# Gated cross-attention and sign FFN: row vectors and gates loaded to every partition by DMA in place of one-row products on TensorE

## The chip, the cores and the metric

One core of one Trainium2 chip runs the kernel. The metric is the device time of one execution in microseconds (us); less is better. The engines are TensorE (PE), VectorE (DVE), ScalarE (ACT), GpSimd (POOL) and SyncE (SP, which only issues transfers here); each runs its own instructions in order and meets the others at semaphores.

## The reference

x is 16 batches of 128 rows of 256 values, ctx has the same shape, all float32. A mask marks keys to leave out.

```python
def block(x, ctx, mask, g_xattn, g_ffn, Wq, bq, Wk, bk, Wo, bo, W, scale, bias):
    q = layernorm(x) @ Wq.T + bq
    k = ctx @ Wk.T + bk
    s = where(mask, -inf, q @ k.T)                 # one head, 128 x 128 per batch
    a = softmax(s) @ ctx                           # the values are ctx itself
    x = x + tanh(g_xattn[0]) * (a @ Wo.T + bo)
    w = where(W >= 0, 1, -1)
    y = clip(layernorm(x) @ w.T * scale + bias, -100, 100)
    return x + tanh(g_ffn[0]) * y
```

The change is about the five small operands: the gates g_xattn and g_ffn (one value each) and the rows bo, scale and bias (256 values each). Each of them is needed in all 128 partitions.

## The kernel before, in words

The 16 batches are worked on in 8 groups of two (G = 8, GB = 2); "(g)" behind a name means group g. Everything stays in SBUF. Each engine's program is written out by hand in one block, so the order on an engine is the order of the code, and a wait holds up everything behind it on that engine.

Set-up. The query and key weights are multiplied into one 256 x 256 matrix (wqk), so that K = wqk applied to ctx is all that the scores need from ctx. wo is transposed on PE and multiplied by tanh(g_xattn) on eviction (woT_hi on ACT, L245; woT_lo on DVE, L478, which waits for woT_hi), so that Z = ctx @ woT replaces the values. The FFN weights become signs with their mean taken off (w_cent, DVE, L495 to L502), and PE transposes them. Operands marked hi and lo are two parts of one float32 value, whose products are added up.

Each group then goes through: transposes of ctx (cT, L533, with the eviction cT_hi on ACT L200 and cT_lo on DVE L380), statistics of x (bn_x, DVE L362, and mv_x, L366), normalisation on POOL (xn, L304), its transposes (xT), K (L538, evicted to K_sb on ACT, L210), Z (L538), scores (a product that lays the mask, L595, then L600), the negated maximum on DVE (nmax, L395), exp on ACT (L221), transposes of p (L608, copied to PT_sb by ACT, L226), attend (L619), the residual on DVE (x1, L405, which the profile lists as x_sb), its statistics and transposes (x1T), the FFN product (L538 into ps_F), scaling on DVE (f_scaled, L413), bias and clip on POOL (f_biased L322, f_clip), and the last addition on DVE.

PE's program, which sets the order around the change: 18 warm-up transposes, the product of the two weights, transpose_ctx(0), the key bias, transpose_x(0), project_K(0), the gate product (L656), the transposes of wo, the bo product (L660). Then for i = 0 to 6: scores(i), transpose_ctx(i+1), transpose_x1(i-1) from i = 1 on, transpose_x(i+1), project_Z(i), project_K(i+1), transpose_p(i), then for i = 0 the transposes of w_cent and the scale and bias products (L675, L676), for later i ffn(i-1), and last attend(i).

The small operands. ACT issues eight loads at its start: bq, bk, the mask, two gates, bo, scale and bias, the last five to partition 0 alone. To bring them to all partitions, PE multiplies a row of 128 ones (ones_1) with each: the gates into o_bank, bo into x1T_bank, scale and bias into the two halves of f_bank. ACT takes them from there: tanh_g (L242), bo_g (L247, times tanh), sc_g and bi_g (L261, L262). Since these products borrow banks that have other uses, there are waits for that too: attend(0) for tanh_ready, the transposes of w_cent for bo_g_ready, the scale product for woT_lo_ready, and ffn(0) for bi_g_ready.

DVE's program around the change: after the set-up of wqk come the statistics of groups 1, 2 and 3, then woT_lo, four operations on one column each that make the clip limits (L480 to L485), and the loop: max_of_scores(0) (nmax), split_cT(1), the w_cent sequence. ACT's: K_sb(0), tanh_g, woT_hi, bo_g, and the loop: cT_hi(1), exp(0), xT(1), Z_sb(0), PT_sb(0), K_sb(1), wT, sc_g, bi_g. POOL waits for bo_g before its first xb = x + bo_g (L316).

SP issues its loads in this order: wq, wk, x(0), ctx(0), x(1), wo, ctx(1), w, and then x and ctx of groups 2 to 7, 256 KB each; later the stores.

Of the kernel before, what the change touches and what calls it, by code (L numbers as in the profile page):

```python
# [21 lines left out]
def gated_xattn_ffn(nc, x, ctx, mask, g_xattn, g_ffn, wq, bq, wk, bk, wo, bo, w_ffn, scale_ffn, bias_ffn, out):  # L22
# [25 lines left out]
    with ExitStack() as stack:  # L48
# [6 lines left out]
        def bank(name):  # L55
# [51 lines left out]

        gate_row, bo_row, sc_row, bi_row = sb("gate_row", [1, 2]), sb("bo_row", [1, D]), sb("sc_row", [1, D]), sb("bi_row", [1, D])
        tanh_g, neg_g, abs_g = sb("tanh_g", [P, 2]), sb("neg_g", [P, 1]), sb("abs_g", [P, 1])
# [7 lines left out]
        sel = sb("sel", [P, G, P], BF16)  # L117
        ones_1 = sb("ones_1", [1, P])

        x_loaded, ctx_loaded = [sem(f"x_loaded{g}") for g in range(G)], [sem(f"ctx_loaded{g}") for g in range(G)]  # L120
        wq_loaded, wk_loaded, bq_loaded, bk_loaded, wo_loaded, w_loaded, gate_loaded, rows_loaded, mask_loaded, stored = (
            sem(n) for n in ("wq_loaded", "wk_loaded", "bq_loaded", "bk_loaded", "wo_loaded", "w_loaded", "gate_loaded",
                             "rows_loaded", "mask_loaded", "stored"))

# [5 lines left out]
                             "wqk_lo_ready"))  # L130
        ps_gate_ready, tanh_ready, ps_rows_ready, ps_bo_ready, bo_g_ready, sc_g_ready, bi_g_ready = (
            sem(n) for n in ("ps_gate_ready", "tanh_ready", "ps_rows_ready", "ps_bo_ready", "bo_g_ready", "sc_g_ready",
                             "bi_g_ready"))
        neg_g_done, abs_g_done, clip_ready = (sem(n) for n in ("neg_g_done", "abs_g_done", "clip_ready"))
# [24 lines left out]
        def _(sp):  # L159
# [11 lines left out]
            sp.dma_start(wo_sb[:], wo.rearrange("(c p) d -> p c d", p=P)).then_inc(wo_loaded, 16)  # L171
            load_ctx(1)
            sp.dma_start(w_sb[:], w_ffn.rearrange("(c p) d -> p c d", p=P)).then_inc(w_loaded, 16)
            for g in range(2, G):
                load_x(g)
                load_ctx(g)
            for g in range(G - 2):
                sp.wait_ge(out_done, g + 1)
                sp.dma_start(out_rows[:, rows(g), :], out_sb[:, rows(g), :]).then_inc(stored, 16)
# [9 lines left out]
        def _(act):  # L189
# [3 lines left out]
            for k, v in enumerate((g_xattn, g_ffn)):  # L193
                act.dma_start(gate_row[:, k:k + 1], row(v)).then_inc(gate_loaded, 16)
            for tile, v in ((bo_row, bo), (sc_row, scale_ffn), (bi_row, bias_ffn)):
                act.dma_start(tile[:], row(v)).then_inc(rows_loaded, 16)

# [42 lines left out]
            evict_K(0)  # L240
            act.wait_ge(ps_gate_ready, 1)
            nc.scalar.activation(tanh_g[:], o_bank[:, 0:2], ACT.Tanh).then_inc(tanh_ready, 1)  # L242
            act.wait_ge(tanh_ready, 1)
            act.wait_ge(ps_woT_ready, 1)
            nc.scalar.activation(woT_hi[:], ps_woT, ACT.Identity, scale=tanh_g[:, 0:1]).then_inc(woT_hi_ready, 1)  # L245
            act.wait_ge(ps_bo_ready, 1)
            nc.scalar.activation(bo_g[:], x1T_bank[:, 0:D], ACT.Identity, scale=tanh_g[:, 0:1]).then_inc(bo_g_ready, 1)  # L247
            for i in range(G - 1):
                evict_cT_hi(i + 1)
                exp(i)  # L250
                if i >= 1:
                    evict_x1T_hi(i - 1)
                evict_xT(i + 1)
                evict_Z(i)
                evict_PT(i)
                evict_K(i + 1)
                if i == 0:
                    act.wait_ge(ps_wT_ready, 1)
                    nc.scalar.copy(wT[:], ps_x1T).then_inc(wT_ready, 1)
                    act.wait_ge(ps_rows_ready, 1)  # L260
                    nc.scalar.activation(sc_g[:], f_bank[:, 0:D], ACT.Identity, scale=tanh_g[:, 1:2]).then_inc(sc_g_ready, 1)  # L261
                    nc.scalar.activation(bi_g[:], f_bank[:, D:2 * D], ACT.Identity, scale=tanh_g[:, 1:2]  # L262
                                         ).then_inc(bi_g_ready, 1)
# [9 lines left out]
        def _(pool):  # L273
            nc.gpsimd.memset(ident[:], 0.0).then_inc(zeroed, 1)
            nc.gpsimd.memset(half[:], -0.5).then_inc(consts_ready, 1)
            nc.gpsimd.memset(ones_1[:], 1.0).then_inc(consts_ready, 1)
            pool.wait_ge(zeroed, 1)
# [50 lines left out]

            pool.wait_ge(consts_ready, 2)
            offsets_x(0)  # L330
# [26 lines left out]
        def _(dve):  # L357
# [49 lines left out]

            def scale_ffn_out(g):
                dve.wait_ge(rstd_1_done, g + 1)
                dve.wait_ge(F_prod, g + 1)  # L410
                for b in range(GB):
                    r = g * GB + b
                    nc.vector.scalar_tensor_tensor(out=f_scaled[:, r], in0=ps_F[:, b], scalar=rstd_1[:, r:r + 1],  # L413
                                                   in1=sc_g[:], op0=ALU.mult, op1=ALU.mult).then_inc(f_scaled_done, 1)
# [113 lines left out]
        def _(pe):  # L528
# [82 lines left out]
            def attend(g):  # L611
                pe.wait_ge(PT_done, g + 1)
                pe.wait_ge(Z_done, g + 1)
                if g >= 1:
                    pe.wait_ge(x1_done, GB * g)
                else:
                    pe.wait_ge(tanh_ready, 1)
                for b in range(GB):
                    last = nc.tensor.matmul(ps_O[:, b], PT_sb[:, g % 2, b], Z_sb[:, g % 2, b], start=True, stop=True)  # L619
                last.then_inc(O_prod, 1)  # L620

            def ffn(g):
# [3 lines left out]
                else:  # L626
                    pe.wait_ge(bi_g_ready, 1)
                for b in range(GB):
# [6 lines left out]
            pe.wait_ge(ident_ready, 1)  # L635
            pe.wait_ge(consts_ready, 2)
            for _ in range(WARM_UP):
# [16 lines left out]
            project_K(0)  # L654
            pe.wait_ge(gate_loaded, 32)
            nc.tensor.matmul(o_bank[:, 0:2], ones_1[:], gate_row[:], start=True, stop=True).then_inc(ps_gate_ready, 1)  # L656
            pe.wait_ge(wo_loaded, 16)
            transposes(ps_woT, wo_sb).then_inc(ps_woT_ready, 1)
            pe.wait_ge(rows_loaded, 48)
            nc.tensor.matmul(x1T_bank[:, 0:D], ones_1[:], bo_row[:], start=True, stop=True).then_inc(ps_bo_ready, 1)  # L660
            for i in range(G - 1):
# [8 lines left out]
                if i == 0:  # L670
                    pe.wait_ge(bo_g_ready, 1)
                    pe.wait_ge(w_cent_ready, DC)
                    transposes(ps_x1T, w_cent).then_inc(ps_wT_ready, 1)
                    pe.wait_ge(woT_lo_ready, 1)
                    nc.tensor.matmul(f_bank[:, 0:D], ones_1[:], sc_row[:], start=True, stop=True)  # L675
                    nc.tensor.matmul(f_bank[:, D:2 * D], ones_1[:], bi_row[:], start=True, stop=True).then_inc(ps_rows_ready, 1)  # L676
                else:
# [53 lines left out]
```

## Time and profile before

| | |
|---|---|
| median of 3 runs | 81.14 us (80.91 to 81.71) |
| the profiled execution, its own time | 81.19 us |
| its span, first to last instruction | 79.3 us |
| PE busy | 69.3 us |
| DVE, POOL, ACT busy | 56.1, 55.0, 36.6 us |
| granted TensorE clock, mean over the span | 0.970 of full speed |

All times in the rows count from the start of the span. In the chain, a piece is as long as it carried the chain, so that overlapping instructions of one engine aren't counted twice; "issue" is time in which nothing shown was waited for. In a timeline, a row merges instructions of one kind that follow each other (x2, x4), its second number is the time from the first's start to the last's end, and the brackets hold the engine's idle time ahead of it and what ended it.

### The profile page before, as it was taken

Reading aid. Unit: us, or ns where it says so; the run is one execution under the profiler, and the core shown is the slowest. Engines: PE = TensorE matmul, PEld = TensorE weight load, DVE = VectorE, ACT = ScalarE, POOL = GpSimd, SP = SyncE. Lnnn points to the kernel's source line nnn. Section 1 sums busy time; section 2 is a strip of 40 time slices with the busy share of each in tenths; the row PEclk is TensorE's granted clock in tenths of the full one; section 3 lists DMA queues with packets and bytes.
Section 4 is the critical chain, followed back from the end, with each engine's and each line's share of the span. In section 5 each row is a group of like instructions: output and inputs, shape, how many; then the busy total and the mean of one; then the engine's idle time right before and its main releaser. Section 6 shows DMA issues by size and latency. Waiting matters only on the chain.

```text
span 79.3 us, 1567 instructions
## 1 busy us (share of the span) xinstructions
PE 69.3 (87%) x522; PEld 64.8 (82%) x522; DVE 56.1 (71%) x163; ACT 36.6 (46%) x99; POOL 55.0 (69%) x102
## 2 busy tenths in 40 slices
PE   2999899999999999999999999999999899865000
PEld 2998797986999899989999998999899798654000
DVE  2494976890469489929966980896498359899980
ACT  0054257748386529435850945394267525330000
POOL 6006576989406508889999988999999994528930
PEclk9999999999999999999999999999999999999755
DMA  2899999980000000040003003000300300300025
GB/s 22 265 368 351 351 349 348 348 254 0 0 4 0 0 0 8 0 134 2 0 4 132 8 0 132 0 0 0 132 0 8 111 22 0 119 13 0 0 72 192
DMA packets 7713, 7.44 MB, mean 94 GB/s; under 512 B 791, under 2 KB 7450, under 8 KB 7706
## 3 DMA queue, kind: packets, MB, share of 16 engines
q1 hardware_dynamic: 7376, 7.34, 28.7%
q8 instruction: 4, 0.07, 0.4%
q10 hardware_dynamic: 330, 0.01, 0.2%
q14 instruction: 3, 0.02, 0.1%
HBM read 5.25 MB, written 2.10 MB: 93 GB/s over the span
## 4 chain that ended last, share of the span: by engine, by line
PE 73%; DVE 12%; DMA 4%; ACT 3%; POOL 3%; issue 2%; DVEq 0%; POOLq 0%
PE ps_K L538 14%; PE ps_Z L538 14%; PE ps_S L600 9%; PE ps_O L619 8%; PE ps_F L538 8%; PE ps_xT L533 5%; PE ps_x1T L533 4%; PE ps_cT L533 4%; DMA wq_sb<-in_L_xattn_Wq_dram 4%; PE ps_S L608 2%; DVE f_biased L439 2%; DVE out_sb L444 2%; DVE f_last L441 1%; POOL xn L304 1%; DVE f_scaled L436 1%
## 5 line engine op out<-in xcount | busy, mean ns | idle before, releaser
L405 DVE SCALAR_TENSOR_TENSOR x_sb<-ps_O,recip_p,xb_sb 128x256 f32<-128x256 f32 x14 | 6.1, 480 | 11.1 <-PE ps_O L619 11.1
L322 POOL TENSOR_TENSOR f_biased<-f_scaled,bi_g 128x256 f32<-128x256 f32 x14 | 10.0, 733 | 3.4 <-DVE f_scaled L413 3.3
L316 POOL TENSOR_TENSOR xb_sb<-x_sb,bo_g 128x256 f32<-128x256 f32 x16 | 11.4, 729 | 0.8 <-ACT bo_g L247 0.8
L200 ACT CAST cT_hi<-ps_cT 128x512 fp32r<-128x512 f32 x8 | 4.7, 586 | 13.5 <-PE ps_cT L533 13.4
L304 POOL TENSOR_SCALAR xn<-x_sb,rstd_x,off_x 128x256 f32<-128x256 f32 x16 | 9.9, 626 | 0.5
L538 PE MATMUL ps_Z<-woT_hi,cT_hi 128*128 128x256 f32 x32 | 9.7, 305 | 0.0
L538 PE MATMUL ps_K<-cT_hi,wqk_hi 128*128 128x256 f32 x32 | 9.1, 283 | 0.0
L538 PE MATMUL ps_K<-cT_hi,wqk_lo 128*128 128x256 f32 x32 | 9.0, 282 | 0.0
L538 PE MATMUL ps_K<-cT_lo,wqk_hi 128*128 128x256 f32 x32 | 9.0, 282 | 0.0
L538 PE MATMUL ps_Z<-woT_lo,cT_hi 128*128 128x256 f32 x32 | 9.0, 281 | 0.0
L538 PE MATMUL ps_Z<-woT_hi,cT_lo 128*128 128x256 f32 x32 | 9.0, 281 | 0.0
L600 PE MATMUL ps_S<-K_sb,xT 128*128 128x128 f32 x64 | 8.5, 276 | 0.2 <-ACT K_sb L210 0.2
L600 PEld LDWEIGHTS ps_S<-K_sb,xT 128*128 128x128 f32 x64 | 7.8, 192 | 1.1 <-issue 0.4
L538 PE MATMUL ps_F<-wT,x1T_hi 128*128 128x256 f32 x28 | 7.6, 303 | 0.1
L309 POOL TENSOR_SCALAR ve<-mv 128x2 f32<-128x2 f32 x8 | 2.4, 297 | 7.3 <-DVE mv L376 6.9
L619 PE MATMUL ps_O<-Z_sb,PT_sb 128*128 128x256 f32 x28 | 7.3, 382 | 0.0
L210 ACT ACTIVATE K_sb<-ps_K,kbias 128x256 f32<-128x256 f32 x16 | 6.7, 477 | 0.9 <-PE ps_K L538 0.9
L413 DVE SCALAR_TENSOR_TENSOR f_scaled<-ps_F,rstd,sc_g 128x256 f32<-128x256 f32 x14 | 6.1, 476 | 1.5 <-PE ps_F L538 1.2
L538 PE MATMUL ps_F<-wT,x1T_lo 128*128 128x256 f32 x28 | 7.0, 282 | 0.0
L221 ACT ACTIVATE p_sb<-ps_S,nmax 128x128 f32<-128x128 f32 x16 | 5.8, 369 | 1.8 <-DVE nmax L395 1.8
L226 ACT COPY PT_sb<-ps_S 128x256 f32<-128x256 f32 x8 | 3.0, 374 | 7.4 <-PE ps_S L608 7.4
L362 DVE BATCH_NORM_STATS2 bn_x<-x_sb 128x6 f32<-128x256 f32 x16 | 5.9, 413 | 0.5 <-DMA x_sb<-in_x_dram 0.5
(126 smaller groups left out, 199.7 us busy)
## 6 DMA issues: line engine op xcount, KB each, us to landing
x_sb<-in_x_dram SPq DMA_DIRECT2D x8, 256.0 KB, 5.8
ctx_sb<-in_ctx_dram SPq DMA_DIRECT2D x8, 256.0 KB, 6.1
out_dram<-out_sb SPq DMA_DIRECT2D x7, 256.0 KB, 2.1
wq_sb<-in_L_xattn_Wq_dram SPq DMA_DIRECT2D x1, 256.0 KB, 2.9
wk_sb<-in_L_xattn_Wk_dram SPq DMA_DIRECT2D x1, 256.0 KB, 3.4
wo_sb<-in_L_xattn_Wo_dram SPq DMA_DIRECT2D x1, 256.0 KB, 4.4
w_sb<-in_L_ffn_weights_dram SPq DMA_DIRECT2D x1, 256.0 KB, 4.9
out_dram<-out_sb SPq DMA_DIRECT2D x2, 128.0 KB, 1.9
```

Source lines behind the costliest of these rows:

```text
L210: nc.scalar.activation(K_sb[:, g % 2, c], ps_K[:, c], ACT.Identity, bias=kbias[:, c:c + 1]).then_inc(K_done, 1)
L221: nc.scalar.activation(p_sb[:, g % 2, b], ps_S[b], ACT.Exp, bias=nmax[:, r:r + 1], accum_out=psum_p[:, r:r + 1]).then_inc(p_done, 1)
L304: nc.gpsimd.tensor_scalar(xn[:, g % 3, b], x_sb[:, r], rstd_x[:, r:r + 1], off_x[:, r:r + 1], ALU.mult, ALU.add).then_inc(xn_done, 1)
L316: nc.gpsimd.tensor_tensor(xb_sb[:, r], x_sb[:, r], bo_g[:], ALU.add).then_inc(xb_done, 1)
L322: nc.gpsimd.tensor_tensor(f_biased[:, r], f_scaled[:, r], bi_g[:], ALU.add).then_inc(f_biased_done, 1)
L362: nc.vector.bn_stats(bn_x[:, r], x_sb[:, r]).then_inc(bn_x_done, 1)
L405: nc.vector.scalar_tensor_tensor(out=x1_sb[:, r], in0=ps_O[:, b], scalar=recip_p[:, r:r + 1], in1=xb_sb[:, r], op0=ALU.mult, op1=ALU.add). ...
L413: nc.vector.scalar_tensor_tensor(out=f_scaled[:, r], in0=ps_F[:, b], scalar=rstd_1[:, r:r + 1], in1=sc_g[:], op0=ALU.mult, op1=ALU.mult).t ...
L533: last = nc.tensor.transpose(dst[:, c, b * P:(b + 1) * P], src[:, b, c * P:(c + 1) * P], ident[:])
L538: last = nc.tensor.matmul(dst, lhsT, rhs, start=(n == 0), stop=(n == len(pairs) - 1))
L600: last = nc.tensor.matmul(ps_S[b], xT[:, g % 2, c, b * P:(b + 1) * P], K_sb[:, g % 2, c, b * P:(b + 1) * P], start=False, stop=(b == GB - ...
L619: last = nc.tensor.matmul(ps_O[:, b], PT_sb[:, g % 2, b], Z_sb[:, g % 2, b], start=True, stop=True)
```

## The change

The five small operands are loaded to all 128 partitions by DMA: the source is the row with a step of 0 over 128 partitions (to_broadcast). The gates stay on ACT's queue, bo goes on SP's behind ctx(1), scale and bias on SP's behind ctx(3). ACT reads the SBUF tiles gate_col, bo_all, sc_all and bi_all where it read PSUM banks. The one-row products, the row of ones and the waits for the borrowed banks go; ffn(0) waits for woT_lo (f_bank still holds the transposes of wo), and DVE's scale_ffn_out waits for sc_g_ready.

```diff
@@ sync
             load_ctx(1)
+            sp.dma_start(bo_all[:], row(bo).to_broadcast([P, D])).then_inc(bo_loaded, 16)
             sp.dma_start(w_sb[:], w_ffn.rearrange("(c p) d -> p c d", p=P)).then_inc(w_loaded, 16)
             for g in range(2, G):
                 load_x(g)
                 load_ctx(g)
+                if g == 3:
+                    for tile, v in ((sc_all, scale_ffn), (bi_all, bias_ffn)):
+                        sp.dma_start(tile[:], row(v).to_broadcast([P, D])).then_inc(sc_bi_loaded, 16)
@@ scalar
             for k, v in enumerate((g_xattn, g_ffn)):
-                act.dma_start(gate_row[:, k:k + 1], row(v)).then_inc(gate_loaded, 16)
-            for tile, v in ((bo_row, bo), (sc_row, scale_ffn), (bi_row, bias_ffn)):
-                act.dma_start(tile[:], row(v)).then_inc(rows_loaded, 16)
+                act.dma_start(gate_col[:, k:k + 1], row(v).to_broadcast([P, 1])).then_inc(gate_loaded, 16)
...
-            act.wait_ge(ps_gate_ready, 1)
-            nc.scalar.activation(tanh_g[:], o_bank[:, 0:2], ACT.Tanh).then_inc(tanh_ready, 1)
+            act.wait_ge(gate_loaded, 32)
+            nc.scalar.activation(tanh_g[:], gate_col[:], ACT.Tanh).then_inc(tanh_ready, 1)
...
-            act.wait_ge(ps_bo_ready, 1)
-            nc.scalar.activation(bo_g[:], x1T_bank[:, 0:D], ACT.Identity, scale=tanh_g[:, 0:1]).then_inc(bo_g_ready, 1)
+            act.wait_ge(bo_loaded, 16)
+            nc.scalar.activation(bo_g[:], bo_all[:], ACT.Identity, scale=tanh_g[:, 0:1]).then_inc(bo_g_ready, 1)
...
-                    act.wait_ge(ps_rows_ready, 1)
-                    nc.scalar.activation(sc_g[:], f_bank[:, 0:D], ACT.Identity, scale=tanh_g[:, 1:2]).then_inc(sc_g_ready, 1)
-                    nc.scalar.activation(bi_g[:], f_bank[:, D:2 * D], ACT.Identity, scale=tanh_g[:, 1:2]
+                    act.wait_ge(sc_bi_loaded, 32)
+                    nc.scalar.activation(sc_g[:], sc_all[:], ACT.Identity, scale=tanh_g[:, 1:2]).then_inc(sc_g_ready, 1)
+                    nc.scalar.activation(bi_g[:], bi_all[:], ACT.Identity, scale=tanh_g[:, 1:2]
@@ gpsimd
-            nc.gpsimd.memset(ones_1[:], 1.0).then_inc(consts_ready, 1)
...
-            pool.wait_ge(consts_ready, 2)
+            pool.wait_ge(consts_ready, 1)
@@ vector, scale_ffn_out(g)
+                dve.wait_ge(sc_g_ready, 1)
@@ tensor
# attend(0)
-                else:
-                    pe.wait_ge(tanh_ready, 1)
# ffn(0)
-                    pe.wait_ge(bi_g_ready, 1)
+                    pe.wait_ge(woT_lo_ready, 1)
# ahead of the warm-up
-            pe.wait_ge(consts_ready, 2)
# behind project_K(0)
-            pe.wait_ge(gate_loaded, 32)
-            nc.tensor.matmul(o_bank[:, 0:2], ones_1[:], gate_row[:], start=True, stop=True).then_inc(ps_gate_ready, 1)
             pe.wait_ge(wo_loaded, 16)
             transposes(ps_woT, wo_sb).then_inc(ps_woT_ready, 1)
-            pe.wait_ge(rows_loaded, 48)
-            nc.tensor.matmul(x1T_bank[:, 0:D], ones_1[:], bo_row[:], start=True, stop=True).then_inc(ps_bo_ready, 1)
...
                 if i == 0:
-                    pe.wait_ge(bo_g_ready, 1)
                     pe.wait_ge(w_cent_ready, DC)
                     transposes(ps_x1T, w_cent).then_inc(ps_wT_ready, 1)
-                    pe.wait_ge(woT_lo_ready, 1)
-                    nc.tensor.matmul(f_bank[:, 0:D], ones_1[:], sc_row[:], start=True, stop=True)
-                    nc.tensor.matmul(f_bank[:, D:2 * D], ones_1[:], bi_row[:], start=True, stop=True).then_inc(ps_rows_ready, 1)
```

## Rows read from the trace of the kernel before

**Rows 1.** Page, part 1: busy time, share of the span, instructions.
```profile
PE 69.3 (87%) x522; PEld 64.8 (82%) x522; DVE 56.1 (71%) x163; ACT 36.6 (46%) x99; POOL 55.0 (69%) x102
```

**Rows 2.** Chain that ended last: start us, us, what.
```profile
5.33 0.71 DVE bn_x L362 x2
...
11.30 0.31 PE ps_O L656 x2
...
12.20 0.62 PE ps_x1T L660 x2
12.82 0.22 PE ps_S L595
13.04 0.89 PE ps_S L600 x8
...
14.80 1.42 PE ps_Z L538 x12
...
17.92 0.63 PE ps_x1T L533 x4
18.55 0.62 PE ps_F L675 x2
19.17 0.43 PE ps_F L676 x2
19.60 1.06 PE ps_O L619 x4
20.66 0.11 PE ps_S L595
...
26.98 0.86 PE ps_O L619 x4
```

**Rows 3.** Timeline of ACT: start us, us, operation, [idle before <-releaser].
```profile
11.40 0.84 ACT L210 ACTIVATE K_sb<-ps_K,kbias 128x256 f32<-128x256 f32 x2 [0.91 <-PE ps_K L538]
12.13 0.17 ACT L242 ACTIVATE tanh_g<-ps_O 128x2 f32<-128x2 f32 x1
12.34 0.69 ACT L245 ACTIVATE woT_hi<-ps_F,tanh_g 128x512 fp32r<-128x512 f32 x1
12.92 0.47 ACT L247 ACTIVATE bo_g<-ps_x1T,tanh_g 128x256 f32<-128x256 f32 x1
14.40 0.59 ACT L200 CAST cT_hi<-ps_cT 128x512 fp32r<-128x512 f32 x1 [1.01 <-PE ps_cT L533]
...
15.49 0.21 ACT L221 ACTIVATION_READ_ACCUMULATOR p_sb<-ps_S,nmax 128x1 f32 x1
```

**Rows 4.** Timeline of DVE, same columns.
```profile
11.31 0.75 DVE L362 BATCH_NORM_STATS2 bn_x<-x_sb 128x6 f32<-128x256 f32 x2 [0.54 <-DMA x_sb<-in_x_dram]
...
13.06 0.75 DVE L478 SCALAR_TENSOR_TENSOR woT_lo<-ps_F,tanh_g,woT_hi 128x512 fp32r<-128x512 f32 x1 [0.78 <-ACT woT_hi L245]
...
14.38 0.42 DVE L395 TENSOR_REDUCE nmax<-ps_S 128x2 f32<-128x258 f32 x1
15.02 0.69 DVE L380 TENSOR_TENSOR cT_lo<-ps_cT,cT_hi 128x512 fp32r<-128x512 f32 x1 [0.22 <-ACT cT_hi L200]
...
17.00 0.76 DVE L502 TENSOR_SCALAR w_cent<-w_sign,w_mean 128x256 f32<-128x256 f32 x2
```

**Rows 5.** Timeline of SP's queue: issues of x(0) and x(3).
```profile
1.62 0.43 SPq L161 DMA_DIRECT2D x_sb<-in_x_dram  x1
...
5.71 0.47 SPq L161 DMA_DIRECT2D x_sb<-in_x_dram  x1
```

**Rows 6.** DMA issues, x(0) and then x(3): KB, us to landing.
```profile
x_sb<-in_x_dram SPq DMA_DIRECT2D x1, 256.0 KB, 3.6
...
x_sb<-in_x_dram SPq DMA_DIRECT2D x1, 256.0 KB, 5.6
```

**Rows 7.** DMA queue of ACT, 3.50 to 4.50: packets, MB, share.
```profile
q10 hardware_dynamic: 156, 0.00, 9.2%
```

**Rows 8.** Timeline of POOL.
```profile
29.87 1.43 POOL L322 TENSOR_TENSOR f_biased<-f_scaled,bi_g 128x256 f32<-128x256 f32 x2 [3.07 <-DVE f_scaled L413]
```

More of the change, by code:

```diff
@@ L106, in gated_xattn_ffn @@
         wT = sb("wT", [P, DC, D], F32R)
-        gate_row, bo_row, sc_row, bi_row = sb("gate_row", [1, 2]), sb("bo_row", [1, D]), sb("sc_row", [1, D]), sb("bi_row", [1, D])
+        gate_col, bo_all, sc_all, bi_all = sb("gate_col", [P, 2]), sb("bo_all", [P, D]), sb("sc_all", [P, D]), sb("bi_all", [P, D])
         tanh_g, neg_g, abs_g = sb("tanh_g", [P, 2]), sb("neg_g", [P, 1]), sb("abs_g", [P, 1])
@@ L117, in gated_xattn_ffn @@
         sel = sb("sel", [P, G, P], BF16)
-        ones_1 = sb("ones_1", [1, P])
         x_loaded, ctx_loaded = [sem(f"x_loaded{g}") for g in range(G)], [sem(f"ctx_loaded{g}") for g in range(G)]
-        wq_loaded, wk_loaded, bq_loaded, bk_loaded, wo_loaded, w_loaded, gate_loaded, rows_loaded, mask_loaded, stored = (
+        wq_loaded, wk_loaded, bq_loaded, bk_loaded, wo_loaded, w_loaded, gate_loaded, bo_loaded, sc_bi_loaded, mask_loaded, stored = (
             sem(n) for n in ("wq_loaded", "wk_loaded", "bq_loaded", "bk_loaded", "wo_loaded", "w_loaded", "gate_loaded",
-                             "rows_loaded", "mask_loaded", "stored"))
+                             "bo_loaded", "sc_bi_loaded", "mask_loaded", "stored"))
         zeroed, ident_ready, consts_ready, mask_filled, place_done, group_of_done, sel_done, mask_ready = (
@@ L130, in gated_xattn_ffn @@
                              "wqk_lo_ready"))
-        ps_gate_ready, tanh_ready, ps_rows_ready, ps_bo_ready, bo_g_ready, sc_g_ready, bi_g_ready = (
-            sem(n) for n in ("ps_gate_ready", "tanh_ready", "ps_rows_ready", "ps_bo_ready", "bo_g_ready", "sc_g_ready",
-                             "bi_g_ready"))
+        tanh_ready, bo_g_ready, sc_g_ready, bi_g_ready = (
+            sem(n) for n in ("tanh_ready", "bo_g_ready", "sc_g_ready", "bi_g_ready"))
         neg_g_done, abs_g_done, clip_ready = (sem(n) for n in ("neg_g_done", "abs_g_done", "clip_ready"))
```

## The prediction

> **What bounds the kernel now.** I read the page first: TensorE (PE) is busy for 87% of the span, more than any other engine [rows 1]. That is an average, so the next view was the chain of waits, read in order of time. Once the first statistics (bn_x at 5.33) have led to PE, it lies on PE almost without a break; rows 2 show the part that the change touches. Two rows in it are no group's work: the gate products (11.30, 0.31 us), and the bo product (12.20, 0.62 us). Two more stand at 18.55 (scale, 0.62) and 19.17 (bias, 0.43). One-row operands don't make them cheap: bo, scale and bias each have a weight load and a stream of 256 columns, in two passes (x2). The row behind them is longer too: attend(0) at 19.60 has 1.06 us where attend(1) at 26.98 has 0.86, and the mask product at 12.82 has 0.22 where the next one at 20.66 has 0.11 [rows 2]. The question is then what PE would wait for if these went. For that I read the timelines of ScalarE (ACT) and VectorE (DVE) beside the same stretch [rows 3, 4], and for the transfers that take their place, SP's issues, their times to landing and the small packets' share [rows 5 to 7].
>
> **The change, step 1: up to the first scores.** Without gates and bo, PE starts the woT transposes at 11.30; they took 0.59 (from 11.30 + 0.31 to 12.20 [rows 2]), so they end at 11.89 at the latest and the mask product by 12.1. But scores(0) needs K_sb, which ACT writes from 11.40 for 0.84 us, to 12.24 [rows 3], and nothing in the change moves that: it follows project_K(0), which ends at 11.30 [rows 2]. With a hop of 0.06 (tanh ends at 12.30 and woT_hi starts at 12.34, so 0.04 is a hop's least [rows 3]) the scores start at 12.30 in place of 13.04: 0.74 us won of the 1.04 that the two products and the slow start of the mask product took (0.31 + 0.62 + 0.11). The rest becomes a wait on ACT.
>
> **Step 2: up to the transposes of w_cent.** PE went from 13.04 to 17.92 in 4.88 us [rows 2], so it could be there at 17.18. What it needs there is w_cent, the end of a DVE sequence. tanh starts at 12.13 because K_sb comes before it on ACT, not because of the gate product; it stays, and so do woT_hi (12.34), woT_lo on DVE (13.06) and, behind woT_lo and four small operations in DVE's order, nmax at 14.38 [rows 3, 4]. (project_Z(0), which needs woT_lo done at 13.81, was reached at 14.80, 1.76 behind the scores [rows 2], and would be at 12.30 + 1.76 = 14.06; it doesn't stall.) Behind nmax stood 0.22 us of waiting for cT_hi(1), which ACT began at 14.40 after 1.01 us of waiting for PE [rows 3, 4]. The context transposes now come 0.74 earlier, so cT_hi(1) is done before 14.4 and that wait goes, with it some 0.06 of hand-over: 0.28. w_cent was done at 17.00 + 0.76 = 17.76 [rows 4] and is done at 17.48. PE starts its transposes at 17.53 rather than 17.92. So of the 0.74 only 0.39 is left here. The exponentials don't interfere: they hang on nmax, which stays, and PE's transposes of p came well behind them (ACT was through with the second at 15.70 [rows 3]).
>
> **Step 3: up to the second group.** The scale and bias products go, 0.62 + 0.43, and attend(0) falls from 1.06 to attend(1)'s 0.86: 1.25 us [rows 2]. What attend(0) needs (the copies of PT and Z on ACT) is made while PE waits for w_cent and transposes it. Sum of the first three steps: 0.39 + 1.25 = 1.64.
>
> **Step 4: what is loaded, and when.** SP's row: x(0) is issued at 1.62 and lands 3.6 later, at 5.22; x(3) at 5.71 and 5.6, at 11.31 [rows 5, 6]. Between them lie eight transfers of 256 KB in 6.09 us: 0.76 each. A broadcast of 128 rows of 1 KB is 128 KB, so 0.38 (estimate; no transfer of before reads one address many times, so this has to be bounded: from 0, since added bytes can't speed anything, to 16 x 0.38 = 6.1 if one DMA engine of 16 did it all). I take 0.38, by the same-sized packets beside it. bo_all stands behind ctx(1), at about 8.3 + 0.4 = 8.7; bo_g reads it at 12.92 [rows 3]. Everything behind it is 0.38 later: x(3) lands at 11.69, and the statistics of group 3, which stand in DVE's order ahead of woT_lo, end later by that; DVE then idled 0.78 before woT_lo [rows 4], which covers it. scale and bias come behind ctx(3), near 12.1 + 1.1 = 13.2, for use after 18; x(4) and later ones are 1.1 late with several us to spare. ACT issues five DMAs in place of eight.
>
> The gates are worse than they look: two loads of 4 bytes to one partition become two of 128 packets of 4 bytes. In 3.50 to 4.50 us, 156 packets of ACT's queue (bk, mask and the like) took 9.2% of the 16 engines [rows 7], 0.09 us; 254 more take 0.15. They are issued from 2.1 us on, and x(0) must come past them. x(0) lands at 5.22 and DVE starts on it at 5.33 [rows 2, 6]; less a hop of 0.06, only 0.05 of cover. And bn_x is on the chain to PE's first work on x. So 0.10 us is lost and carried through all later steps. Ends: 0, if they pass after x(0), and 0.70, if such a packet takes as long as one of 1 KB (254 of them 0.75, less 0.05). I take 0.10, since rows 7 are packets of nearly the same kind. The Trainium skill speaks against this part: "DMA: Bandwidth & Descriptors", Specifications, holds that a transfer under 512 B is below line rate because the engine reads, modifies and writes. It gives no time per packet; the row of the trace agrees in direction (0.00 MB to two decimals, and yet 9.2% of the engines' time), and by the rule alone the loss would lie anywhere up to my upper end.
>
> **After 20.66.** The chain holds no transfer, and ScalarE, VectorE and GpSimd (POOL) hang on PE's results: even POOL, full from 29.87 on, starts there after 3.07 us of waiting for f_scaled [rows 8], so it moves as one with PE. New waits there (sc_g on DVE) are long met. I expect a plain shift to the end.
>
> **Sum.** 1.64 - 0.10 = 1.54 us. The profiled execution took 81.19 (79.3 span and 1.89 around it): 79.65. The runs' median is 0.05 lower, so 79.6. Own range: 79.3 to 80.0, from 0.35 us of doubt on w_cent and the gates. One per cent, about what a measurement of this kernel can tell from no change, is 0.81 us.
>
> **Rivals.**
> A, *all of it comes off*: 1.98 of products, 0.20 and 0.11 of slow starts behind them, 2.29: 78.9. For it: PE is the chain. Against: K_sb and w_cent end too late [rows 3, 4]. It would need DVE's order to run ahead by itself. 0.06.
> B, *the products were partly cover*: PE's idle time moves. If cT_hi(1) gives DVE nothing, w_cent stays at 17.76 and PE starts at 17.82: 0.10 + 1.25 - 0.10 = 1.25, 79.9; if the tiny packets also cost 0.70, 0.65 is left: 80.5. For it: both waits are close. 0.20, three parts of it under 80.3.
> C, *slower, through the broadcast*: bo_all's read of one address by 128 packets is slow, and SP's queue is in order, so x(3) is late by L. DVE can't pass its statistics, woT_lo comes L - 0.78 late, and with it nmax, w_cent and PE. It eats the gain at L = 0.78 + 1.54 = 2.32, six times the 0.38 estimated. Shared by two engines, L = 3.0: 81.9; on one, L = 6.1: 84.9. For it: nothing in the trace bounds it. Against: the destination's 128 partitions are as in x, where all engines share. 0.07. Of this the Trainium skill ("DMA: Bandwidth & Descriptors", Rules for kernel authors) says that a leading zero-step dimension of fewer than 16 copies confines a transfer to so many engines; here it has 128 copies, so by that rule all 16 work, and no row of before shows it.
> D, *given back later*: the shift meets another bound (POOL in mid-run, where it is nearly full) and 0.3 or less is left: 80.9. Against: POOL's wait in rows 8. 0.07.
> Forecast: 0.60.
>
> **Numbers.** Faster by over 1% (under 80.3): forecast 0.60, A 0.06, three quarters of B, 0.15, less a rest for the forecast's own misses: 0.77. Slower by over 1%: C's greater part, 0.06. Within: 0.17. Range: 79.0 (A is left out) to 80.9, with B and most of D in it; C is out.
>
> **What would show it.** Right: PE's chain without the four rows; a wait of 0.2 to 0.45 before scores(0), ended by ACT's K_sb at 12.3; a wait of about 0.35 before the transposes of w_cent, ended by DVE; attend(0) near 0.86; the second group's mask product at 19.1 and not 20.66; after that the old times less the shift (attend(1) at 25.4); bn_x of group 0 near 5.4; x(3)'s statistics near 11.7. Wrong: bn_x(3) past 12.5 (C), bn_x(0) past 5.8 (B), woT_lo or nmax off their old times, or a first f_biased on POOL that hasn't moved by what PE has (D).

## The result and the profile after

The changed kernel takes 83.09 us (median of 4 runs, 82.93 to 84.06), the kernel before in the same session 81.25: a ratio of 1.0247 (95% interval 1.0153 to 1.0341). It is slower by 1.8 us, where 1.5 us less was forecast, and the whole interval lies on the slower side. The profiled execution took 83.03, with a span of 81.2. Ratios here and below are of undisturbed executions only.

The page of the changed kernel, its first, second and fourth parts: PE has 2.1 us less work than in [rows 1], and the work is not what sets the end. There are 10% of the chain in one load of x, and the moved GB/s have a hole in the third to fifth slice (4 to 10 us), where before they stood at 348 to 368 from the third slice to the eighth.

```profile
PE 67.2 (83%) x514; PEld 63.3 (78%) x514; DVE 57.0 (70%) x163; ACT 36.8 (45%) x99; POOL 55.0 (68%) x101
...
DMA  1868899998100000003003003000210020210015
GB/s 18 275 192 279 302 344 362 353 348 269 45 4 0 0 0 0 0 13 128 0 4 116 13 0 120 18 0 0 74 55 8 32 97 0 72 58 0 0 61 198
...
PE 59%; DVE 16%; DMA 10%; SPq 7%; ACT 3%; issue 2%
```

The chain of the changed kernel, for comparison with [rows 2]:

```profile
6.91 8.14 DMA x_sb<-in_x_dram
...
15.08 0.75 DVE bn_x L362 x2
15.83 0.22 DVE mv_x L366 x2
16.04 0.63 DVE woT_lo L479
...
17.18 0.33 DVE nmax L395
17.52 0.60 DVE cT_lo L380
...
18.48 0.70 DVE w_sum L498
...
19.48 1.53 DVE w_cent L503 x2
...
21.05 0.66 PE ps_x1T L534 x4
21.71 0.86 PE ps_O L618 x4
22.57 0.11 PE ps_S L596
...
28.91 0.87 PE ps_O L618 x4
```

The reader is to see this: the chain no longer comes to the scores over PE. It waits until 15.05 for x(3), goes through DVE's statistics to woT_lo at 16.04 (before: 13.06 in the timeline of DVE [rows 4]), nmax, cT_lo and the w_cent sequence, and comes to PE only at 21.05 with the transposes of w_cent (before: 17.92). There the scale and bias products are missing as forecast, attend(0) has its 0.86, and the mask product stands at 22.57, 1.91 later than 20.66. From there all is the old chain (attend(1) at 28.91 against 26.98, 1.93 later), and the span is 1.9 longer.

A view gives the time from issue to landing to 0.1 us, so differences of two landings here and below are good to about 0.1. The DMA issues of the changed kernel: x(0), ctx(0), ctx(1), bo and w, in this order, with KB and the us from issue to landing, to be read with [rows 6]. They are issued at 1.63, 2.10, 3.64, 4.15 and 4.66.

```profile
x_sb<-in_x_dram SPq DMA_DIRECT2D x1, 256.0 KB, 3.6
...
ctx_sb<-in_ctx_dram SPq DMA_DIRECT2D x1, 256.0 KB, 5.4
...
ctx_sb<-in_ctx_dram SPq DMA_DIRECT2D x1, 256.0 KB, 6.3
...
bo_all<-in_L_xattn_bo_dram SPq DMA_DIRECT2D x1, 128.0 KB, 7.9
...
w_sb<-in_L_ffn_weights_dram SPq DMA_DIRECT2D x1, 256.0 KB, 8.1
```

x(0) lands at 5.23, as before (5.22). ctx(0), next in the queue, lands at 7.5; it used to land at 5.99. ctx(1) lands at 9.94 (8.22), and between it and w at 12.76 lie 2.82 us, for 384 KB that should take 1.14 at the 0.76 per 256 KB of [rows 5, 6]. So there are two slow places ("holes" below): one behind x(0), in which 1.7 us are lost, and one at bo, in which another 1.7 go. x(3) lands at 6.91 + 8.1 = 15.0, 3.7 late. The windows of the changed kernel show them as stretches in which the DMA engines are little busy and move half the bytes (the last two columns):

```profile
4.50:5.50 1.00, 1.00 (x7) 0.94 (x6) 0.86 (x4) 0.00 (x0) 0.00 (x0) 1.00 0.58 163
5.50:6.50 1.00, 1.00 (x5) 0.64 (x4) 0.79 (x4) 0.00 (x0) 0.03 (x1) 1.00 0.59 167
...
7.50:8.50 1.00, 0.93 (x6) 0.89 (x7) 0.34 (x2) 0.23 (x1) 0.78 (x3) 1.00 1.04 360
...
9.50:10.50 1.00, 1.00 (x11) 1.00 (x11) 1.00 (x4) 0.25 (x3) 0.00 (x0) 1.00 0.74 259
```

and those of the kernel before at the same places:

```profile
4.50:5.50 1.00, 1.00 (x7) 1.00 (x6) 0.95 (x4) 0.65 (x1) 0.00 (x0) 1.00 1.07 372
...
9.50:10.50 1.00, 1.00 (x11) 1.00 (x10) 1.00 (x6) 0.58 (x1) 0.44 (x2) 1.00 1.10 347
```

### The profile page after: what moved, and what is told of

Its sections match the earlier page's. It is cut to its first block, busy times and chain, and to the rows that moved or that the text cites. A ratio compares the mean times of both kernels' runs of the same rounds, so it can differ in the third digit from the quotient of the medians.

```text
span 81.2 us, 1548 instructions
## 1 busy us (share of the span) xinstructions
PE 67.2 (83%) x514; PEld 63.3 (78%) x514; DVE 57.0 (70%) x163; ACT 36.8 (45%) x99; POOL 55.0 (68%) x101
## 4 chain that ended last, share of the span: by engine, by line
PE 59%; DVE 16%; DMA 10%; SPq 7%; ACT 3%; issue 2%
PE ps_Z L539 12%; PE ps_K L539 11%; DMA x_sb<-in_x_dram 10%; PE ps_S L601 8%; PE ps_O L618 7%; PE ps_F L539 7%; PE ps_x1T L534 4%; PE ps_xT L534 3%; PE ps_cT L534 3%; SPq L159 2%; SPq L162 2%; DVE w_cent L503 2%; DVE f_biased L440 2%; DVE out_sb L445 2%; PE ps_S L609 2%
## 5 line engine op out<-in xcount | busy, mean ns | idle before, releaser
L539 PEld LDWEIGHTS ps_Z<-woT_hi,cT_hi 128*128 128x128 f32 x32 | 6.0, 188 | 2.1 <-DVE woT_lo L479 2.1
```

The lines of the kernel that those rows point to most:

```text
L539: last = nc.tensor.matmul(dst, lhsT, rhs, start=(n == 0), stop=(n == len(pairs) - 1))
```

## The experiments

Two theories to begin with. S: reading the same address of HBM 128 times is slow. T: small packets and added bytes are slow, wherever they read. Each experiment is a change to the changed kernel.

**Different places in place of one.** The loads get 128 sources of the same size.

```diff
-                act.dma_start(gate_col[:, k:k + 1], row(v).to_broadcast([P, 1])).then_inc(gate_loaded, 16)
+                act.dma_start(gate_col[:, k:k + 1], bk.rearrange("(k p o) -> k p o", k=2, o=1)[k]).then_inc(gate_loaded, 16)
...
-            sp.dma_start(bo_all[:], row(bo).to_broadcast([P, D])).then_inc(bo_loaded, 16)
+            sp.dma_start(bo_all[:], x_rows[:, 0, :]).then_inc(bo_loaded, 16)
... (scale and bias likewise, from batches 1 and 2 of x)
```

all_distinct (both edits):

> The changed kernel, but each of the five loads takes 128 different places of HBM in place of one: both gates 128 consecutive values of bk (4 bytes each, so packets as small as before), bo, scale and bias the 128 rows of x of batches 0, 1 and 2 (1 KB each). Same bytes, same packets, same queues; gates and rows have other values, so the output is another. Theory S (same address: what is slow is that one place of HBM is read 128 times): ctx(0) lands near 6.1 us of the span and x(3) near 11.7, the scores start at 12.3, w_cent is transposed near 17.5 and the time is the one first forecast, 79.6 (79.3 to 80.0). Rival T (tiny packets and added bytes are slow by themselves, wherever they read): as the changed kernel, ctx(0) at 7.5, x(3) at 15.0, 83.1.

gates_distinct (the first alone):

> The changed kernel with only the two gate loads taking 128 different 4-byte places (values of bk), so the gates have other values. Theory S: ctx(0) lands near 6.1 in place of 7.5, x(3) near 13.3 in place of 15.05 (bo's broadcast still costs about 1.6 over its bytes), time about 81.2. Rival T: nothing changes, ctx(0) at 7.5, 83.1.

rows_distinct (the second alone):

> The changed kernel with only bo, scale and bias taken from 128 different rows of x (other values in them); the gates are broadcast from one address. Theory S: ctx(0) still lands near 7.5, x(3) near 13.4, time about 81.2. Rival T: no change in x(3), 15.0, and 83.1.

gates_pe (gates by the product on PE, all lines of it as before the change):

> The changed kernel with the gates loaded to one partition and spread by the product on TensorE as before; bo, scale and bias stay broadcasts. Both theories: ctx(0) near 6.0, x(3) near 13.3, about 81.1, since PE waits for K_sb anyway and the gate product costs nothing there. If the gate loads are not the cause of the first slow stretch (4.5 to 7.5 us), x(3) stays at 15.0 and the time at 83.1.

Measured, as ratios to the kernel before: all_distinct 0.9913 (0.9890 to 0.9936), 80.54 us; gates_distinct 0.9903 (0.9882 to 0.9924), 80.62; rows_distinct 1.0011 (0.9975 to 1.0047), 81.38 in the profiled execution; gates_pe 0.9889 (0.9869 to 0.9909), 80.39.

Neither theory stands as it was. all_distinct is 0.9 us above what S expected and 2.5 below T's 83.1. Without the one address, the gates alone bring 2.5 us back and the rows alone 1.7, but both together no more than the gates alone, so the two holes don't simply add up. For bo, S holds: read from different places, it takes 0.3 to 0.4 us (w lands 1.1 behind ctx(1) in all six kernels with such rows, 0.76 of it its own); from one address it takes 1.0 to 2.4, in eight kernels. The windows of all_distinct show no second hole, but nearly the whole first one:

```profile
4.50:5.50 1.00, 1.00 (x7) 1.00 (x6) 0.90 (x4) 0.00 (x0) 0.00 (x0) 1.00 0.57 166
5.50:6.50 1.00, 0.99 (x5) 0.53 (x4) 0.71 (x4) 0.00 (x0) 0.12 (x1) 1.00 0.70 177
...
8.50:9.50 1.00, 1.00 (x10) 0.95 (x10) 0.78 (x2) 0.56 (x2) 0.63 (x2) 1.00 1.10 375
```

and those of gates_pe next to nothing of the first hole (4.50 to 5.50 has 304 GB/s there), but the second:

```profile
5.50:6.50 1.00, 1.00 (x4) 0.82 (x4) 0.72 (x4) 0.00 (x0) 0.10 (x1) 1.00 1.05 357
...
7.50:8.50 1.00, 1.00 (x8) 0.90 (x7) 0.93 (x4) 0.62 (x2) 0.81 (x3) 1.00 0.78 152
8.50:9.50 1.00, 1.00 (x11) 1.00 (x10) 1.00 (x3) 0.50 (x2) 0.69 (x2) 1.00 0.80 212
```

So the first hole belongs to the gate loads, and consecutive places in 512 bytes help them only in part (ctx(1) lands at 9.63 and 9.12, against 9.94 and 10.54 with one address, and 9.04 in gates_pe).

**What makes the gate loads slow?** Four kernels, all with rows from different places.

gates_8b (two more copies of the bk load):

> Rows from 128 different places as in all_distinct (other values in bo, scale and bias), and the two gate loads replaced by two more copies of the bk load: 128 packets of 8 bytes each, at the same place in ACT's queue (gates have other values). Theory Z (4 bytes are below what the path handles at speed; 8 are not, since bq and bk ran 156 packets a microsecond): no dip between 4.5 and 7.0 us, ctx(0) near 6.1, x(3) near 11.7, time 79.6 to 79.9. Theory Q (it is the fourth and fifth load in that queue, among transfers that by now fill the engines, that are slow, whatever their size): as all_distinct, ctx(0) at 7.4, x(3) at 13.1, 80.5.

gates_early (the gate broadcasts ahead of bk and the mask on ACT's queue):

> Rows from 128 different places again (other values in them), gates broadcast from one address as in the changed kernel, but issued second and third on ACT's queue, ahead of bk and the mask. Compare with rows_distinct (81.4 profiled, ctx(0) at 8.1, x(3) at 13.9). Theory Z: the dip comes with the 4-byte packets, now near 3 to 5 us, and x(0), which heads the chain, may land later too, by up to 1: 81.4 or more. Theory Q: the dip stays at 4.5 to 7 us but belongs to bk's packets; x(3) near 13.1, about 80.6. Should the gates be through before the queue of SP is full, there is no dip: 79.7.

gates_512b:

```diff
+                act.dma_start(gate_col[:, k], x_rows[:, k, 0:P]).then_inc(gate_loaded, 16)
```

> all_distinct (rows from 128 different places, other values in them), with each of the two gate loads made 512 bytes to each partition, from 128 different rows of x (64 KB each, at the same place in ACT's queue, other values in the gates). Theory P (what costs is a small packet, 50 to 90 ns of a DMA engine each): no dip beyond the 0.37 us of the bytes, ctx(0) at 6.0 to 6.4, x(3) near 12.1, about 79.7. Theory Q (a further load of 128 packets on ACT's queue beside SP's is slow, whatever its size): ctx(0) at 7.0 or later, x(3) at 13 or later, 80.4 or more.

gates_far:

```diff
+                act.dma_start(gate_col[:, k:k + 1], x_rows[:, k, 0:1], allow_slow_non_contiguous=True).then_inc(gate_loaded, 16)
```

> all_distinct with the 4 bytes of each gate packet read 1 KB apart (first value of 128 rows of x) instead of side by side in 512 bytes. Theory P: same dip as all_distinct, 4.5 to 7.0 us, ctx(0) at 7.0 to 7.4, x(3) at 13.0, 80.5. Theory N (the dip comes from many reads near one place of HBM): no dip, ctx(0) near 6.1, x(3) at 11.8, 79.6.

Measured: gates_8b 0.982 (0.976 to 0.988), ctx(1) at 9.64; gates_early 1.0038 (1.0004 to 1.0072), x(0) itself at 7.22 and ctx(1) at 10.12; gates_512b 0.9883 (0.9851 to 0.9915), ctx(1) at 9.64, 0.37 of it bytes; gates_far 0.9825 (0.9745 to 0.9906), ctx(1) at 8.74. gates_far ran only twice, with 79.39 us in the profiled execution and 80.44 in the other, which is as slow as gates_512b (80.32 and 80.45). Without any such load ctx(1) lands between 8.13 and 9.14, at 8.6 in the mean of seven profiles. The windows of gates_far:

```profile
4.50:5.50 1.00, 1.00 (x7) 1.00 (x6) 0.96 (x4) 0.00 (x0) 0.00 (x0) 1.00 0.93 286
5.50:6.50 1.00, 0.89 (x5) 0.44 (x3) 0.63 (x4) 0.07 (x1) 0.19 (x1) 1.00 1.07 328
```

In this profile the same 256 packets of 4 bytes, 1 KB apart, cost the others next to nothing (286 and 328 GB/s, where one address leaves 163 and 167). So size alone is not it, which ends P; P had also expected gates_512b to lose no more than its bytes. 8 bytes from bk, side by side and a third time, are slow again, which ends Z. gates_early shows that being early doesn't help: the hole moved to 3.5 to 5.5 us and took x(0), which heads the chain, with it. Its windows:

```profile
3.50:4.50 1.00, 1.00 (x6) 1.00 (x6) 0.71 (x2) 0.91 (x1) 0.00 (x0) 1.00 0.43 112
4.50:5.50 1.00, 1.00 (x6) 0.71 (x4) 0.83 (x4) 0.00 (x0) 0.00 (x0) 1.00 0.42 128
```

Q doesn't fit the profile of gates_far, which stands at the same place of the same queue, but it does fit gates_512b and gates_8b. By ctx(1) against the mean of 8.6, one address costs 1.3 to 1.9, 128 places within 512 bytes or 1 KB 0.5 to 1.0, places 1 KB apart 0.1 (gates_far) and, less its bytes, 0.7 (gates_512b). One address is thus the worst in four profiles of four, also by the time of gates_far's two executions against rows_distinct (0.9825 against 1.0011). That the cost falls with the distance of the places is not shown: it hangs on one landing, and gates_512b, with the same distance, speaks against it. That bk and bq, of the near kind, cost nothing visible as the first two loads is not explained either.

**Is it the first touch, the tensor, or the order?** The first three are changes to gates_pe; before_again is the kernel before once more.

rows_touched (the three 1 KB loads to one partition are back on ACT's queue, unused):

> gates_pe (gates by the product, bo, scale, bias broadcast) with the three 1 KB loads of bo, scale and bias to one partition put back on ACT's queue, unused, ahead of the broadcasts. In gates_pe bo's broadcast brought a dip (7.0 to 9.0 us; ctx(1) and w land 2.2 apart, where a plain 128 KB and 256 KB take 1.1), but scale's and bias's brought none. Theory F (the first reading of a place is slow, and 128 packets then wait for it): the dip goes, w lands 1.1 to 1.3 behind ctx(1), x(3) near 12.3, time near 80.0. Rival S (128 reads of one address are slow each time): as gates_pe, 2.2 apart, x(3) at 13.5, 80.4 to 81.0.

bo_twice:

> gates_pe with bo's broadcast issued twice in a row (the second into a spare tile). Theory F: the second costs its bytes, 0.37: w lands about 2.6 behind ctx(1). Rival S: the second costs as the first, 1.1 to 1.5: w lands 3.3 to 3.7 behind ctx(1).

rows_swapped (scale_ffn for bo in the first broadcast, bo for scale_ffn in the second):

> gates_pe with the first broadcast (behind ctx(1)) reading scale and the second (behind ctx(3)) reading bo; the third still reads bias. bo and scale hold each other's values. Theory A (the tensor: bo's place in HBM is the slow one): w lands 1.1 to 1.2 behind ctx(1), and x(4) 2.2 or more behind ctx(3), where gates_pe had 1.46. Rival O (the order: the first broadcast is slow, because the 16 engines come to it in step, and later ones are not, whatever they read): w 2.2 or more behind ctx(1), x(4) 1.5 behind ctx(3), as gates_pe.

before_again:

> The kernel before once more, for how far landings differ between executions: ctx(0) at 6.0 and x(3) at 11.3 in the first profile. If these are steady to 0.2, the 7.0 of ctx(0) in gates_pe has a cause in that kernel; if ctx(0) moves by up to 1, single landings can't be read to better than that.

Measured: in rows_touched w lands 3.15 behind ctx(1), where F expected 1.1 to 1.3. Its five executions took 80.30 to 81.90, and the profiled one is the slowest; but the fastest three, 80.30 to 80.50, are no faster than gates_pe either (ratio 0.9884 against 0.9889), where F expected 80.0. So F falls. In bo_twice (85.64, profiled, and 83.30) it is 5.21, or 2.2 for each of the two beyond w's 0.76: S. In rows_swapped (82.31, profiled, and 80.47) the scale row at the first place is slow too (3.12), and bo at the second is (x(4) 2.9 behind ctx(3)); but scale and bias at the second place are not, in any of the six kernels that broadcast them there (x(4) 1.4 to 1.8 behind ctx(3), where the bytes alone give 1.52). So neither the tensor nor the order alone decides, as far as the one profile of rows_swapped goes, which is of the slower of its two executions; why scale and bias are spared stays open. So does what makes the same broadcast cost 1.0 in one profile and 2.4 in another.

before_again: ctx(0) at 5.80 and x(3) at 11.41, within 0.2 of the first profile, time 1.0001 (0.9984 to 1.0017). Landings behind a hole are less steady: gates_pe had ctx(0) at 7.0 and rows_touched at 6.1 with nothing different ahead of it. Differences under 1 us between gate variants are therefore weak.

**How does the lateness reach the end?** stats_later moves DVE's wait for x(3) behind cT_lo(1):

```diff
-            stats_x(2)
-            stats_x(3)
...
                 split_cT(i + 1)
                 if i == 0:
+                    stats_x(2)
+                    stats_x(3)
```

> The changed kernel, with DVE's statistics of groups 2 and 3 moved behind split_cT(1), so that woT_lo, nmax and cT_lo(1) no longer stand behind the late x(3). If the late x(3) does its harm through DVE's order: woT_lo near 13.6, nmax near 14.9, both ahead of the changed kernel's 15.96 and 17.10; the statistics then end near 17.4 and w_cent near 19.6 instead of 21.0: 1.4 less, 81.7. If the harm goes another way (POOL's offsets, PE's own loads): 83.0 or above.

Measured: 1.0083 (1.0043 to 1.0124), profiled 82.35: 0.7 to 1.0 us less than the changed kernel, where 1.4 was expected. nmax starts at 15.72 in place of 17.10 with x(3) as late as ever (14.87), the mask product of the second group at 21.76 in place of 22.57. So the path was DVE's order. The gain is smaller than expected because woT_lo came at 14.36 and not 13.6, since ctx(0), and with it ACT's woT_hi, was late as well; what follows in DVE's order was late by as much (w_cent ended at 20.35 and not 19.6).

**A version without either hole.** late_rows:

```diff
-            sp.dma_start(bo_all[:], row(bo).to_broadcast([P, D])).then_inc(bo_loaded, 16)
...
                 if g == 3:
+                    sp.dma_start(bo_all[:], row(bo).to_broadcast([P, D])).then_inc(bo_loaded, 16)
+                if g == 5:
                     for tile, v in ((sc_all, scale_ffn), (bi_all, bias_ffn)):
@@ scalar: bo_g (L247 of before) behind evict_Z(0); sc_g and bi_g under i == 1
@@ gpsimd, behind norm_x(1); the same two calls are skipped later, under i == 0
+            offsets_x(2)
+            norm_x(2)
             pool.wait_ge(bo_g_ready, 1)
@@ gates: row load and one-row product, as in the kernel before
```

> Same result as the reference. Gates by the product on TensorE as before (hidden in the wait for K_sb), bo broadcast behind ctx(3), scale and bias behind ctx(5), so that nothing that DVE or PE waits for early stands behind them; bo_g on ACT moved behind Z_sb(0), sc_g and bi_g to the second group; POOL normalises x(2) ahead of its wait for bo_g. If steps 1 to 3 of the forecast are right and late transfers are all that went wrong: x(3) lands at 11.3, w_cent transposed near 17.55, second group's mask product near 19.1, 79.6 (79.3 to 80.0). If the products had other cover than seen: 80.4 as gates_pe, or more.

Measured: 79.65 us (79.50 to 80.03), 0.979 (0.975 to 0.983), faster than both. x(3) lands at 11.67. Its chain, and one row of its DVE timeline:

```profile
11.33 0.31 PE ps_O L664 x2
11.64 0.59 PE ps_F L541 x4
12.22 0.11 PE ps_S L603
12.33 0.08 issue
12.41 1.13 PE ps_S L608 x8
...
17.27 0.22 PE ps_S L616 x2
17.49 0.50 PE ps_x1T L541 x4
17.99 1.09 PE ps_O L627 x4
19.08 0.11 PE ps_S L603
...
25.38 0.87 PE ps_O L627 x4
```

```profile
16.66 0.61 DVE L510 TENSOR_SCALAR w_cent<-w_sign,w_mean 128x256 f32<-128x256 f32 x2
```

Here the forecast can be read line by line. The times of its milestones are met: scores at 12.41 with the gate product still in (12.30 was forecast without it, and gates_far, which has no gate product, is there at 12.29, after 0.54 us of waiting for K_sb); w_cent's transposes at 17.49 (17.53); the two products behind them are gone; the mask product at 19.08 (19.1), attend(1) at 25.38 (25.4).

What lies between them was not as forecast, and part of the agreement is luck. The scores took 1.13 us of the chain behind their wait, where they had 0.89 before (there they had begun at 12.87, under the mask product, which is no longer beside them), so PE was only 0.39 ahead at the next transposes (13.54 against 13.93), not 0.63 or more. w_cent was ready at 17.27, before PE came for it: the wait of about 0.35 for it didn't happen, here or in gates_far, and PE's own work sets 17.49. And attend(0) has 1.09, not 0.86, so the 0.20 that was to come off it stayed. w_cent's transposes took 0.50 in place of 0.63. The sum comes out at 1.58 (20.66 to 19.08) for the 1.64 forecast.

bo's broadcast is as slow as elsewhere (x(4) lands about 2.0 behind ctx(3), for 1.14 of bytes), but nothing that is needed soon stands behind it.

## Why the prediction was wrong

The forecast of 79.6 was 3.5 us off. Steps 1 to 3, the work on PE, gave 1.64, and that sum was right; step 4, the loads, failed. If steps 1 to 3 and the path behind a late x(3) are right, a kernel's profiled time is 81.19 - 1.64, plus what x(3) lands later than 11.31 + 0.78 (nothing, if it is earlier), plus what w_cent takes over its 0.76 (less, if under it). The landing and w_cent's length are read from each profile, nothing is fitted:

| kernel | x(3) lands | w_cent, us | worked out | measured |
|---|---|---|---|---|
| changed kernel | 15.05 | 1.52 | 83.3 | 83.03 |
| rows_swapped | 14.34 | 1.52 | 82.6 | 82.31 |
| rows_touched | 13.89 | 1.52 | 82.1 | 81.90 |
| rows_distinct | 13.90 | 0.73 | 81.3 | 81.38 |
| gates_pe | 13.49 | 1.12 | 81.3 | 81.03 |
| gates_distinct | 13.12 | 0.72 | 80.5 | 80.52 |
| all_distinct | 13.06 | 0.73 | 80.5 | 80.54 |
| gates_512b | 13.02 | 0.72 | 80.4 | 80.32 |
| gates_8b | 12.99 | 0.62 | 80.3 | 80.02 |
| gates_far | 12.16 | 0.62 | 79.5 | 79.39 |
| late_rows | 11.67 | 0.61 | 79.4 | 79.50 |

Eleven kernels agree to 0.3 us over a spread of 3.6. (Not in the table: gates_early, where x(0) is late, stats_later, which has another order, bo_twice, which lost clock.) So the cover of 0.78 that DVE had before woT_lo, the path through DVE's order and the plain shift to the end were as forecast. In the last three rows PE hardly waited for w_cent or not at all, so the w_cent column stands for no wait there. gates_far and late_rows, whose x(3) came within the cover or near it, thus confirm the sum of 1.64, but not the wait in step 2: the longer scores took what the wait was to take.

Step 4 failed, in both of its terms and in what it left out.
- The gates were priced by rows 7: 156 packets for 9.2% of the engines' time, so 254 for 0.15. The row counts the time in which a packet is at work, about 9 ns; it doesn't count what the others wait while many packets read one place. In the first hole all queues together kept the engines 58 and 59% busy. Against the 0.10 forecast, the two gate loads cost 1.3 to 1.9 us of queue time (ctx(1) in the four profiles with one address). Even the upper end that I gave, 0.75, took a packet's own time as its cost.
- The harm was looked for at x(0), for which 0.05 of cover was counted. x(0) landed at 5.23, untouched. All behind it was hit, and what the gates' delay does at x(3) was not asked: only bo's 0.38 was set against the cover of 0.78 there, while x(3) came 3.74 late, 2.96 more than the cover.
- bo was taken at 0.38, by transfers of the same size. That was the wrong likeness, and the text said that nothing in the trace bounds it. Measured 1.0 to 2.4 (2.0 in the changed kernel).
- Rival C had the mechanism, its path through x(3), DVE's statistics and woT_lo, its price (L - 0.78), its point of decision (2.32; the L measured is 3.74) and its sign (bn_x(3) past 12.5; it started at 15.08). It had only bo's broadcast as the cause, though, and nearly half of L, 1.7 us, is the gates'. It was given 0.07, with the number of engines as its only measure. The Trainium skill ("DMA: Bandwidth & Descriptors", Rules for kernel authors) ties a slow broadcast to a short outermost dimension; with 128 copies it was slow all the same, so that rule, rightly applied, spoke for the wrong case.
- Rival B's 0.70 for the gates was the right direction and too small; A and D did not come: PE did wait, and nothing was given back after the second group.

The last 0.76 of the changed kernel are w_cent, 1.52 us for two operations that took 0.76. Two operations on POOL stand beside it in the timeline, the xb additions that were behind it before. That they are the cause is argued from the profiles (last section), and no run was made to test it:

```profile
19.38 1.46 POOL L316 TENSOR_TENSOR xb_sb<-x_sb,bo_g 128x256 f32<-128x256 f32 x2
```

## What to carry to other kernels

A broadcast load can cost several times a plain load of its size (here up to 2.4 us for 128 KB): until it is measured, price it by such a bound, and issue it behind everything that is needed soon. When a load is put into a full, ordered queue, ask which engine waits for the last load behind it, and what stands behind that wait in the engine's own order; the cover there (0.78 us here) is the whole allowance. A one-row product that fills a wait for another engine costs next to nothing (the gates: the scores start at 12.41 with it and at 12.29 without), one that overhangs it costs all of its time (scale and bias: from the end of w_cent's transposes to the mask product it was 2.11 us with them and is 1.09 without), and the chain with the timelines of two engines beside it was enough to tell them apart. And a wait costs more than its length: the scores behind it took 0.24 us more of the chain, which the sum of a forecast should hold.

## What had not been expected of the hardware

- Tiny reads of one place of HBM slow the other transfers too: while two loads of 128 packets of 4 bytes read one address each, all queues together moved 163 to 167 GB/s in place of 371; from places side by side, 166 to 259 in three profiles; with the same packets 1 KB apart, 286 to 328 in the one profile of it.
- w_cent's two operations on DVE (L502 of before) took 1.52 in place of 0.61 to 0.76 in the four profiles in which POOL's additions (TENSOR_TENSOR, xb) had begun some 0.1 us ahead of them, and 1.12 in gates_pe, where POOL began between the two. In late_rows, where POOL began behind the start of both, they took 0.61. The cause itself was not tested.
- Late loads can cost PE its clock, as one execution shows. In bo_twice PE had nothing to do from about 14.4 to 17.6 us, waiting for woT_lo, and the granted clock fell from 2.4 to 1.2 GHz. Windows of bo_twice (the granted clock is the third column from the end) and its chain:

```profile
14.00:16.00 2.00, 0.39 (x4) 0.15 (x2) 1.03 (x5) 0.57 (x1) 0.91 (x2) 1.00 1.06 334
16.00:17.00 1.00, 0.00 (x0) 0.00 (x0) 1.00 (x5) 0.00 (x0) 0.00 (x0) 0.97 1.09 369
17.00:18.00 1.00, 0.40 (x2) 0.40 (x3) 0.93 (x6) 0.00 (x0) 0.91 (x2) 0.50 1.10 367
...
22.00:23.00 1.00, 1.00 (x7) 1.00 (x6) 0.00 (x0) 0.00 (x0) 0.85 (x2) 0.50 0.04 15
...
24.00:25.00 1.00, 1.00 (x7) 0.80 (x6) 0.00 (x0) 1.00 (x3) 0.00 (x0) 1.00 0.00 0
```

```profile
17.60 2.93 PE ps_Z L544 x12
20.53 2.56 PE ps_K L544 x12
...
27.42 1.42 PE ps_Z L544 x12
28.84 1.44 PE ps_K L544 x12
```

The first Z and K products took 2.93 and 2.56 us, the next ones, at full clock, 1.42 and 1.44; the execution took 85.64 us. The clock came back between 23 and 24 us. The Trainium skill ("TensorE: Matmul & The Clock Gate", Part 1) has the same two levels and says that idleness brings the lower one; the trace agrees. The changed kernel's own four executions hold one of 84.06 with a mean clock of 0.927 against 0.976 to 0.983 in the others.
